# Attention kernel on one core: probabilities transposed by DMA, one per row tile, after the division, instead of by TensorE before it

## The chip, the cores and the metric

One Trainium2 chip, one NeuronCore of it. The metric is the device time of one execution in microseconds; of several runs the median is told. PE is TensorE, DVE VectorE, ACT ScalarE, POOL GpSimd and SP SyncE.

## The reference

For each of B = 8 images x of C = 128 channels and 32 x 32 = 1024 positions:

```python
h = group_norm(x, gn_w, gn_b)                     # 32 groups, eps 1e-5
hf = h.reshape(Bn, Cn, Hn * Wn)
q = jnp.einsum('bcn,oc->bno', hf, wq) + bq
k = jnp.einsum('bcn,oc->bon', hf, wk) + bk[None, :, None]
v = jnp.einsum('bcn,oc->bno', hf, wv) + bv
alpha = jnp.einsum('bnc,bcm->bnm', q, k) / jnp.sqrt(jnp.float32(Cn))
alpha = jax.nn.softmax(alpha, axis=-1)
out = jnp.einsum('bnm,bmc->bnc', alpha, v)
out = jnp.einsum('bnc,oc->bon', out, wo) + bo[None, :, None]
return out.reshape(Bn, Cn, Hn, Wn) + x
```

All in fp32.

## The kernel before

The weights are folded once: wq and wk into one matrix (u = its product with h), wo and wv into another (v already holds the output projection). Every fp32 operand of a large product is split into a high and a low fp16 part, and a product is three fp16 matmuls (high by high, high by low, low by high).

The scores of an image are 8 row tiles of 128 queries by 1024 keys (`TILES`); T = 8b + n numbers them over the launch, 64 in all. Four tiles are a group (`GT`), whose value products share one PSUM bank O. The steps of a tile:

- `logits` (PE, L470 to L474): six matmuls of 512 columns into S, one of two PSUM buffers.
- `tile_max` (DVE, L818): adds the keys' and queries' bias to S, writes the negative logits to SBUF and the row minimum (so the maximum) to exp_bias.
- `exponentials` (ACT, L669): exp into probs (fp32, two buffers in SBUF), the row sum beside it. The probabilities are not divided yet.
- `transposes` (PE, L534): eight fp32 transpositions of 128x128 from probs into the PSUM buffers pT0 and pT1.
- `high_parts` (ACT, L682) and `low_parts` (DVE, L828): from PSUM to the fp16 parts pT_hi and pT_lo, 512 columns at a time.
- `values` (PE, L497 to L499): six matmuls of 512 columns per step and four steps to a group, one group behind the tile.

The division comes at the end. `reciprocals` (DVE, L839 and L842) inverts the sums of four tiles at once; SP writes the 128x4 inverses to DRAM (L237) and reads them back broadcast over the partitions (L243); `result` on POOL multiplies (L367), then adds the residual xres (L375). For the last half group DVE does both (L946, L950).

Per image the other engines also make the next image's operands: DVE the statistics (`channel_stats`, L757, `group_spread`, `variance_out`, `group_affine`) and h itself (`normalise`, L804), POOL the split of h (L326, L329), of u (L336, L339), of v with c_tok (L346, L351, L354) and the residual (L358), ACT the copies of u, v and the products out of PSUM (L633, L643, L652).

There is no scheduler: each engine's program is written out in the order in which it runs, one `batch` per image with the steps hung on the tile number j, and semaphores (`wait_ge`) hold an instruction until its operands are there. DVE's order within a batch, for a tile j (shortened):

```python
tile_max(b, p, j + 1, first and j == 0)
if j == 0 and not first:
    reciprocals(b - 1, 1 - p, 1, second)
if j == 1 and not last:
    group_spread(b + 1, 1 - p)
...
    low_parts(b, j)
if j == 5:
    reciprocals(b, p, 0, first)
```

On every engine but SP the row maximum, exponential and logits of a tile stand one tile ahead of the transposition and split. SP issues all DMAs but two.

## Time and profile before

| | |
|---|---|
| median of 3 runs | 270.89 us (269.74 to 270.96) |
| profiled execution, its own time | 269.27 us |
| its span, first to last instruction | 267.5 us |
| PE busy | 254.0 us, 95% |
| DVE, ACT, POOL busy | 209.4, 176.3, 166.6 us |
| granted TensorE clock, mean | 0.995 |
| DMA traffic | 13.06 MB |

The span is what the trace covers. Busy is the time in which an engine works on an instruction; a matmul's end is modelled, so that busy PE is not PE at its peak. An instruction that is held inside its engine, by a port for instance, counts as busy for the whole of its time. Where an engine sat idle, the profile names what ended the wait.

### The profile page before, as it was taken

Reading aid. Unit: us, or ns where it says so; the run is one execution under the profiler, and the core shown is the slowest. Engines: PE = TensorE matmul, PEld = TensorE weight load, DVE = VectorE, ACT = ScalarE, POOL = GpSimd, SP = SyncE. Lnnn points to the kernel's source line nnn. Section 1 sums busy time; section 2 is a strip of 40 time slices with the busy share of each in tenths; the row PEclk is TensorE's granted clock in tenths of the full one; section 3 lists DMA queues with packets and bytes.
Section 4 is the critical chain, followed back from the end, with each engine's and each line's share of the span. In section 5 each row is a group of like instructions: output and inputs, shape, how many; then the busy total and the mean of one; then the engine's idle time right before and its main releaser. Section 6 shows DMA issues by size and latency. Waiting matters only on the chain.

```text
span 267.5 us, 5033 instructions
## 1 busy us (share of the span) xinstructions
PE 254.0 (95%) x1599; PEld 157.5 (59%) x1599; DVE 209.4 (78%) x403; ACT 176.3 (66%) x338; POOL 166.6 (62%) x182
## 2 busy tenths in 40 slices
PE   1979999999999999999999999999999999999992
PEld 1736555665666566566656666566556656665581
DVE  2757978988789778987789779887798788767742
ACT  2438777668666767677667767767776676767650
POOL 4047196545979099763988279772997359790621
PEclk9999999999999999999999999999999999999997
DMA  4202002130033102320033100420030200201034
GB/s 124 73 0 81 1 0 76 46 78 2 0 104 96 39 2 30 130 78 0 0 79 114 46 0 8 149 60 18 0 72 12 74 0 2 79 39 42 0 81 116
DMA packets 9808, 13.06 MB, mean 49 GB/s; under 512 B 3905, under 2 KB 4673, under 8 KB 9793
## 3 DMA queue, kind: packets, MB, share of 16 engines
q1 hardware_dynamic: 9504, 12.75, 17.1%
q14 instruction: 10, 0.07, 0.2%
q10 hardware_dynamic: 288, 0.13, 0.2%
q8 instruction: 6, 0.10, 0.2%
HBM read 8.65 MB, written 4.23 MB: 48 GB/s over the span
## 4 chain that ended last, share of the span: by engine, by line
PE 89%; DMA 4%; ACT 3%; DVE 2%; issue 1%; ACTq 0%; POOL 0%; DVEq 0%
PE pT L534 20%; PE S L470 10%; PE S L472 10%; PE S L474 10%; PE O L499 10%; PE O L498 10%; PE O L497 10%; PE misc L417 2%; PE misc L416 2%; PE misc L415 2%; ACT probs L669 2%; DMA wk_sb<-in_L_conv_wk_dram 2%; DMA inv_rows<-inv_line 1%; ACT pT_hi L682 1%; DMA inv_line<-row_inv 1%
## 5 line engine op out<-in xcount | busy, mean ns | idle before, releaser
L828 DVE SCALAR_TENSOR_TENSOR pT_lo<-pT,pT_hi 128x512 f16<-128x512 f32 x128 | 82.8, 684 | 21.4 <-ACT pT_hi L682 21.4
L682 ACT ACTIVATE pT_hi<-pT 128x512 f16<-128x512 f32 x128 | 69.5, 596 | 36.2 <-PE pT L534 35.5
L818 DVE TENSOR_SCALAR_CACHE_REDUCE neg_logits<-S,c_tok 128x1024 f32<-128x1024 f32 x64 | 81.8, 1279 | 13.3 <-POOL c_tok L346 8.0
L669 ACT ACTIVATE probs<-neg_logits,exp_bias 128x1024 f32<-128x1024 f32 x64 | 73.8, 1153 | 5.8 <-DVE neg_logits L818 5.7
L534 PE MATMUL pT<-ident,probs 128*128 128x128 f32 x512 | 66.7, 273 | 2.5 <-ACT probs L669 2.0
L534 PEld LDWEIGHTS pT<-ident,probs 128*128 128x128 f32 x512 | 58.9, 141 | 14.3 <-ACT probs L669 4.4
L497 PE MATMUL O<-pT_hi,v_hi 128*128 128x512 f16 x120 | 45.5, 379 | 0.0
L498 PE MATMUL O<-pT_lo,v_hi 128*128 128x512 f16 x120 | 45.5, 379 | 0.0
L499 PE MATMUL O<-pT_hi,v_lo 128*128 128x512 f16 x120 | 45.5, 379 | 0.0
L326 POOL TENSOR_TENSOR h_hi<-h,zero 128x512 f16<-128x512 f32 x14 | 14.6, 1041 | 47.0 <-DVE h L804 47.0
L470 PE MATMUL S<-h_hi,u_hi 128*128 128x512 f16 x128 | 38.5, 382 | 0.1
L472 PE MATMUL S<-h_lo,u_hi 128*128 128x512 f16 x128 | 38.5, 383 | 0.0
L474 PE MATMUL S<-h_hi,u_lo 128*128 128x512 f16 x128 | 38.4, 382 | 0.0
L367 POOL TENSOR_TENSOR attn<-av,inv_rows 128x512 f32<-128x512 f32 x15 | 23.3, 1555 | 6.9 <-DMA inv_rows<-inv_line 6.9
L336 POOL TENSOR_TENSOR u_hi<-u,zero 128x512 f16<-128x512 f32 x15 | 15.6, 1040 | 12.3 <-ACT u L633 12.3
L474 PEld LDWEIGHTS S<-h_hi,u_lo 128*128 128x128 f16 x128 | 12.6, 99 | 15.4 <-issue 0.6
L472 PEld LDWEIGHTS S<-h_lo,u_hi 128*128 128x128 f16 x128 | 12.6, 98 | 15.5 <-issue 0.6
L354 POOL TENSOR_TENSOR v_lo<-v,v_hi 128x384 f16<-128x384 f32 (+1 forms) x24 | 19.4, 809 | 1.9
L351 POOL TENSOR_TENSOR v_hi<-v,zeros 128x384 f16<-128x384 f32 (+1 forms) x24 | 20.4, 850 | 0.0
L375 POOL TENSOR_TENSOR y<-attn,xres 128x512 f32<-128x512 f32 x15 | 19.1, 1274 | 2.0
L497 PEld LDWEIGHTS O<-pT_hi,v_hi 128*128 128x128 f16 x120 | 11.7, 98 | 14.3 <-DVE pT_lo L828 2.3
L499 PEld LDWEIGHTS O<-pT_hi,v_lo 128*128 128x128 f16 x120 | 11.7, 98 | 14.2
(119 smaller groups left out, 313.3 us busy)
## 6 DMA issues: line engine op xcount, KB each, us to landing
inv_rows<-inv_line SPq DMA_DIRECT2D x16, 256.0 KB, 3.8
out_dram<-y SPq DMA_DIRECT2D x15, 256.0 KB, 2.0
x_sb<-in_x_dram SPq DMA_DIRECT2D x7, 512.0 KB, 3.3
x_sb<-in_x_dram SPq DMA_DIRECT2D x2, 256.0 KB, 3.6
inv_line<-row_inv SPq DMA_DIRECT2D x16, 2.0 KB, 1.4
out_dram<-y SPq DMA_DIRECT2D x2, 128.0 KB, 1.9
wq_sb<-in_L_conv_wq_dram ACTq DMA_DIRECT2D x1, 64.0 KB, 3.5
wk_sb<-in_L_conv_wk_dram ACTq DMA_DIRECT2D x1, 64.0 KB, 4.1
```

What stands on the lines that cost most here:

```text
L367: nc.gpsimd.tensor_tensor(by_tile(attn[:, q, :]), by_tile(av[:, q, :]), inverses(q), ALU.mult).then_inc(attn_done, 1)
L470: nc.tensor.matmul(s[:, c], q_hi, h_hi[:, p, c], start=True, stop=False)
L472: nc.tensor.matmul(s[:, c], q_hi, h_lo[:, p, c], start=False, stop=False)
L474: last = nc.tensor.matmul(s[:, c], q_lo, h_hi[:, p, c], start=False, stop=True)
L497: nc.tensor.matmul(O[:, :], vh, ph, start=(m == 0), stop=False)
L498: nc.tensor.matmul(O[:, :], vh, pl, start=False, stop=False)
L499: last = nc.tensor.matmul(O[:, :], vl, ph, start=False, stop=(m == TILES - 1))
L534: last = nc.tensor.transpose(pT[half][:, t, :], probs[:, n % 2, m * 128:(m + 1) * 128], ident[:, :])
L669: nc.scalar.activation(probs[:, n % 2, :], neg_logits[:, n % 2, :], ACT.Exp, scale=-1.0, bias=exp_bias[:, p, n:n + 1], accum_out=row_sum[: ...
L682: nc.scalar.activation(pT_hi[:, g, half * GT:(half + 1) * GT, n % GT, :], pT[half][:, :, :], ACT.Copy, scale=P_SCALE).then_inc(hi_done, 1)
L818: nc.vector.tensor_scalar(neg_logits[:, n % 2, :], S[n % 2][:, :], c_tok[:, p, n:n + 1], None, ALU.add, ALU.min, accum_out=exp_bias[:, p, ...
L828: nc.vector.scalar_tensor_tensor(out=pT_lo[:, g, ms, n % GT, :], in0=pT[half][:, :, :], scalar=P_SCALE, in1=pT_hi[:, g, ms, n % GT, :], op ...
```

## The change

The kernel is written anew in the parts around the probabilities; the head, the weights' folding and the three-matmul split stay.

- Removed: `transposes` and both pT buffers in PSUM, `spread_inverse` (32 DMAs), the product with the inverses on POOL, the loops (`Fori`); every engine's program is written out for all 8 images.
- `exponentials` as before. After it DVE's `inverse` scales the tile's row sum by 1/4096 and inverts it (128x1 each), ACT's `high_part` multiplies the tile by it into fp16 and DVE's `low_part` takes the rest, all from SBUF to SBUF over 1024 elements, into `parts`, one of four buffers of 128x2048 fp16.
- SP issues one transposing DMA per tile, 512 KB, from `parts` into `pT` (four groups), and `values` waits for the four of its group (`tr_in`), 7 tiles behind the logits (`LAG`).
- `low_part` lags one tile, `inverse` none. probs and neg_logits keep two buffers each.
- h of the next image is made on POOL, in `h_parts`. `result` on POOL is one addition. O and the bank for small products (M, before misc) are two each.

```diff
-            def transposes(b, n, first):
-                    for t in range(GT):
-                        m = half * GT + t
-                        last = nc.tensor.transpose(pT[half][:, t, :], probs[:, n % 2, m * 128:(m + 1) * 128],
-                                                   ident[:, :])
...
+            def transpose(b, n):
+                T = TILES * b + n
+                g = T // GT
+                eng.wait_ge(lo_done, T + 1)
+                if n % GT == 0 and g >= 4:
+                    eng.wait_ge(av_done, GT * (g - 3))
+                eng.dma_start_transpose(pT[:, g % 4, :, n % GT, :], parts[:, T % SPLITS, :]).then_inc(tr_in[n], 16)
...
+            def high_part(b, n):
+                T, p = TILES * b + n, b % 2
+                act.wait_ge(inv_done, T + 1)
+                if T >= SPLITS:
+                    act.wait_ge(tr_in[(T - SPLITS) % TILES], 16 * ((T - SPLITS) // TILES + 1))
+                nc.scalar.activation(parts[:, T % SPLITS, 0:N], probs[:, n % 2, :], ACT.Copy,
+                                     scale=row_inv[:, p, n:n + 1]).then_inc(hi_done, 1)
...
+            def inverse(b, n):
+                T, p = TILES * b + n, b % 2
+                dve.wait_ge(exp_done, T + 1)
+                nc.vector.tensor_scalar(scaled_sum[:, p, n:n + 1], row_sum[:, p, n:n + 1], 1.0 / P_SCALE, None,
+                                        ALU.mult).then_inc(sum_step, 1)
+                dve.wait_ge(sum_step, T + 1)
+                nc.vector.reciprocal(row_inv[:, p, n:n + 1], scaled_sum[:, p, n:n + 1]).then_inc(inv_done, 1)
+
+            def low_part(b, n):
+                T, p = TILES * b + n, b % 2
+                dve.wait_ge(hi_done, T + 1)
+                nc.vector.scalar_tensor_tensor(out=parts[:, T % SPLITS, N:2 * N], in0=probs[:, n % 2, :],
+                                               scalar=row_inv[:, p, n:n + 1], in1=parts[:, T % SPLITS, 0:N],
+                                               op0=ALU.mult, op1=ALU.subtract).then_inc(lo_done, 1)
...
+            for b in range(B):
+                for n in range(TILES):
+                    row_max(b, n)
+                    if n or b:
+                        low_part(b - (n == 0), (n - 1) % TILES)
...
+                    if n == 6 and b + 2 < B:
+                        channel_stats(b + 2)
+                        aggregate(b + 2)
+                    inverse(b, n)
...
+                nc.gpsimd.tensor_scalar(h[:, cols], x_sb[:, p, cols], ga[:, p:p + 1], gc[:, p:p + 1],
+                                        ALU.mult, ALU.add).then_inc(h_made, 1)
```

VectorE in the middle of an image before (L818 is the row maximum, L828 the low parts of the tile before it, L839 and L842 the inverses of four tiles):

```order
L818 TENSOR_SCALAR neg_logits,exp_bias<-S0,c_tok 128x1024 [waits exp_done,c_done,qk_done]
L828 SCALAR_TENSOR_TENSOR pT_lo<-pT0,pT_hi 128x4x128 [waits hi_done]
L828 SCALAR_TENSOR_TENSOR pT_lo<-pT1,pT_hi 128x4x128 [waits hi_done]
L839 TENSOR_SCALAR scaled_sum<-row_sum 128x4 [waits line_out0,exp_done]
L842 RECIPROCAL row_inv<-scaled_sum 128x4 [waits inv_step]
L818 TENSOR_SCALAR neg_logits,exp_bias<-S1,c_tok 128x1024 [waits exp_done,qk_done]
```

VectorE at the same place now (L698 is the row maximum, L714 the low part, L705 and L708 the inverse):

```order
L698 TENSOR_SCALAR neg_logits,exp_bias<-S0,c_tok 128x1024 [waits exp_done,qk_done]
L714 SCALAR_TENSOR_TENSOR parts<-probs,row_inv,parts 128x1024 [waits hi_done]
L705 TENSOR_SCALAR scaled_sum<-row_sum 128x1 [waits exp_done]
L708 RECIPROCAL row_inv<-scaled_sum 128x1 [waits sum_step]
L698 TENSOR_SCALAR neg_logits,exp_bias<-S1,c_tok 128x1024 [waits exp_done,c_done,qk_done]
L714 SCALAR_TENSOR_TENSOR parts<-probs,row_inv,parts 128x1024 [waits hi_done]
```

The two low parts of 512 have become one of 1024 whose first input is probs in SBUF, and the inverse stands behind every tile, where it waits for the exponential of the same tile; the next row maximum stands behind it.

ScalarE now, in the second image (L567 is the exponential, L578 the high part, L540 a copy of v):

```order
L578 ACTIVATE parts<-probs,row_inv 128x1024 [waits tr_in3,inv_done]
L567 ACTIVATE probs,row_sum<-neg_logits,exp_bias 128x1024 [waits lo_done,bias_done]
L540 COPY v<-M1 128x387 [waits v_done,v_mm]
L555 ACTIVATE ln_var<-var_eps 128x1 [waits var_out]
L557 ACTIVATE rstd0<-ln_var 128x1 [waits ln_step]
L578 ACTIVATE parts<-probs,row_inv 128x1024 [waits tr_in4,inv_done]
```

The high part of a tile stands ahead of the next exponential and waits for the tile's inverse and for the transposing DMA that read its buffer four tiles ago.

## Rows read from the trace of the kernel before

**Rows 1.** The page: span, and busy time, share and instructions of engines.

```profile
span 267.5 us, 5033 instructions
...
PE 254.0 (95%) x1599; PEld 157.5 (59%) x1599; DVE 209.4 (78%) x403; ACT 176.3 (66%) x338; POOL 166.6 (62%) x182
```

**Rows 2.** The page: chain that ended last, shares of the span by engine.

```profile
PE 89%; DMA 4%; ACT 3%; DVE 2%; issue 1%; ACTq 0%; POOL 0%; DVEq 0%
```

**Rows 3.** Busy time of each engine in a stretch in the middle.

```profile
core 0: us, PE busy (x) PEld busy (x) DVE busy (x) ACT busy (x) POOL busy (x), PEclk, DMA share, GB/s
124.00:155.00 31.00, 31.00 (x199) 19.03 (x198) 26.20 (x51) 21.58 (x41) 21.61 (x23) 1.00 0.19 51
```

**Rows 4.** Groups: busy us, mean ns of one | idle before, releaser.

```profile
L534 PE MATMUL pT<-ident,probs 128*128 128x128 f32 x512 | 66.7, 273 | 2.5 <-ACT probs L669 2.0
...
L757 DVE BATCH_NORM_STATS2 bn<-x_sb 128x6 f32<-128x512 f32 x15 | 9.7, 681 | 0.2 <-DMA x_sb<-in_x_dram 0.2
```

**Rows 5.** Timeline of one tile: start us, us, engine, what [idle before].

```profile
129.44 1.28 DVE L818 TENSOR_SCALAR_CACHE_REDUCE neg_logits<-S,c_tok 128x1024 f32<-128x1024 f32 x1 [1.34 <-POOL c_tok L346]
...
131.85 1.12 DVE L839 TENSOR_SCALAR scaled_sum<-row_sum 128x4 f32<-128x4 f32 x1
133.01 0.18 DVE L842 RECIPROCAL row_inv<-scaled_sum 128x4 f32<-128x4 f32 x1
...
131.79 1.16 POOL L339 TENSOR_TENSOR u_lo<-u,u_hi 128x512 f16<-128x512 f32 x1
...
130.85 1.15 ACT L669 ACTIVATE probs<-neg_logits,exp_bias 128x1024 f32<-128x1024 f32 x1 [0.46 <-DVE neg_logits L818]
131.91 0.19 ACT L669 ACTIVATION_READ_ACCUMULATOR probs<-neg_logits,exp_bias 128x1 f32 x1
```

**Rows 6.** Timeline, DVE and POOL around the two halves of h.

```profile
123.72 0.55 DVE L804 TENSOR_SCALAR h<-x_sb,ga,gc 128x512 f32<-128x512 f32 x1
...
125.98 0.92 DVE L804 TENSOR_SCALAR h<-x_sb,ga,gc 128x512 f32<-128x512 f32 x1
...
125.46 1.16 POOL L329 TENSOR_TENSOR h_lo<-h,h_hi 128x512 f16<-128x512 f32 x1
```

**Rows 7.** DVE instructions with two SBUF inputs: group of h_lo; timeline around spread.

```profile
L902 DVE TENSOR_TENSOR h_lo<-h,h_hi 128x512 f16<-128x512 f32 x2 | 1.3, 690 | 0.2 <-ACT h_hi L721 0.2
...
114.27 0.89 POOL L354 TENSOR_TENSOR v_lo<-v,v_hi 128x384 f16<-128x384 f32 x1
115.00 0.22 DVE L771 SCALAR_TENSOR_TENSOR spread<-dmean,mv 128x1 f32<-128x1 f32 x1
...
145.64 0.22 DVE L771 SCALAR_TENSOR_TENSOR spread<-dmean,mv 128x1 f32<-128x1 f32 x1
```

**Rows 8.** Groups of POOL that the change removes or that price what it adds.

```profile
L326 POOL TENSOR_TENSOR h_hi<-h,zero 128x512 f16<-128x512 f32 x14 | 14.6, 1041 | 47.0 <-DVE h L804 47.0
...
L367 POOL TENSOR_TENSOR attn<-av,inv_rows 128x512 f32<-128x512 f32 x15 | 23.3, 1555 | 6.9 <-DMA inv_rows<-inv_line 6.9
```

**Rows 9.** Timeline of DVE: first row maximum, last scaled sum, last y.

```profile
17.26 1.28 DVE L818 TENSOR_SCALAR_CACHE_REDUCE neg_logits<-S,c_tok 128x1024 f32<-128x1024 f32 x1 [2.63 <-POOL c_tok L346]
...
256.67 0.17 DVE L839 TENSOR_SCALAR scaled_sum<-row_sum 128x4 f32<-128x4 f32 x1 [0.33 <-ACT probs L669]
...
264.75 0.43 DVE L950 TENSOR_TENSOR y<-attn,xres 128x256 f32<-128x256 f32 x1
```

**Rows 10.** DMA: the queue (packets, MB, share); issues (KB each, us to landing).

```profile
q1 hardware_dynamic: 9504, 12.75, 17.1%
...
inv_rows<-inv_line SPq DMA_DIRECT2D x16, 256.0 KB, 3.8
...
x_sb<-in_x_dram SPq DMA_DIRECT2D x7, 512.0 KB, 3.3
```

More of the change, by code:

```diff
@@ L287, in _ @@
                               y[:, 1, cols]).then_inc(y_out[1], 16)
-            for q in range(2):
-                eng.wait_ge(line_out[q], 16 * B)
             for q in range(2):
@@ L340, in u_parts, with v_parts @@
                                         ALU.subtract).then_inc(u_done, 1)
-            def v_parts(b, p, part, first):
+            def v_parts(b, part):
+                p = b % 2
                 t0, n = V_PARTS[part]
@@ L347, in v_parts @@
                                         cb[:, :].to_broadcast([128, n]), ALU.add).then_inc(c_done, 1)
-                if part == 0 and not first:
+                if part == 0 and b >= 2:
                     eng.wait_ge(av_done, TILES * (b - 1))
@@ L398, in _ @@
[L398 to L409 removed]
+            v_parts(0, 0)
@@ new lines, in _ @@
+            eng.wait_ge(ob_out, 1)
+            residual(0)
+            for b in range(B):
+                v_parts(b, 1)
+                u_parts(b, 1)
+                if b + 1 < B:
+                    h_parts(b + 1, 0)
+                if b >= 1:
+                    result(b - 1, 0)
+                if b + 1 < B:
+                    h_parts(b + 1, 1)
+                v_parts(b, 2)
+                if b + 1 < B:
+                    u_parts(b + 1, 0)
+                    v_parts(b + 1, 0)
+                if b >= 1:
+                    result(b - 1, 1)
+                if b + 1 < B:
+                    if b >= 1:
+                        eng.wait_ge(y_done, 2 * b)
+                    residual(b + 1)
@@ L412, in _ @@
+            result(B - 1, 0)
         @block.tensor
@@ L439, in project_v @@
                 t0, n = V_PARTS[part]
+                if part or b:
+                    pe.wait_ge(v_out, NV * b + part)
+                if part == 1:
+                    pe.wait_ge(h_ready, 2 * b + 2)
                 for k in range(n):
                     tok = slice((t0 + k) * 128, (t0 + k + 1) * 128)
-                    last = split_product(bank[:, k * VW:(k + 1) * VW], h_hi[:, p, tok], h_lo[:, p, tok],
+                    last = split_product(M[1][:, k * VW:(k + 1) * VW], h_hi[:, b % 2, tok], h_lo[:, b % 2, tok],
@@ L457, in logits @@
                         pe.wait_ge(u_done, 2 * b + 1)
-                if n == 1 and first:
+                if n == 1 and b == 0:
                     pe.wait_ge(u_done, 1)
@@ L463, in logits @@
                     pe.wait_ge(u_done, 2 * b + 2)
-                if not first:
+                if T >= 2:
                     pe.wait_ge(bias_done, T - 1)
@@ L500, in values @@
[L500 to L514 removed]
+                    vh, vl = v_hi[:, p, m, 0:C], v_lo[:, p, m, 0:C]
@@ new lines, in values, with last_values @@
+                    ph, pl = (pT[:, 2 * p + q, part * TILES + m, :, :].rearrange("p t n -> p (t n)")
+                              for part in range(2))
+                    nc.tensor.matmul(O[q][:, :], vh, ph, start=(m == 0), stop=False)
+                    nc.tensor.matmul(O[q][:, :], vh, pl, start=False, stop=False)
+                    last = nc.tensor.matmul(O[q][:, :], vl, ph, start=False, stop=(m == TILES - 1))
+                last.then_inc(av_done, 1)
+            def last_values(half):
+                bank = (M[0], O[1])[half]
+                if half == 0:
+                    pe.wait_ge(u_out, 2 * B - 1)
+                else:
+                    pe.wait_ge(av_out, 2 * B - 2)
+                for t in range(GT // 2):
+                    pe.wait_ge(tr_in[GT + half * GT // 2 + t], 16 * B)
+                for m in range(TILES):
@@ L515, in last_values @@
                     vh, vl = v_hi[:, 1, m, 0:C], v_lo[:, 1, m, 0:C]
-                    ph, pl = (a[:, 1, m, LAST[half], :].rearrange("p t n -> p (t n)") for a in (pT_hi, pT_lo))
+                    ph, pl = (pT[:, 3, part * TILES + m, LAST[half], :].rearrange("p t n -> p (t n)")
+                              for part in range(2))
                     o = bank[:, 0:GN // 2]
```

552 lines of the change are left out of this document (190 added, 362 removed).

## The prediction

> **What bounds the kernel now.** I read the page's busy shares first: PE is busy 254.0 of 267.5 us, DVE 209.4, POOL 166.6 [rows 1]. The chain of waits agrees, with 89% of its time on PE [rows 2]. A stretch in the middle shows PE busy 31.00 of 31.00 us at full granted clock [rows 3]. So PE sets the pace: from the first row maximum at 17.26 to the last exponential's end, just before 256.67, 64 row tiles take 239.4 us, 3.74 us each [rows 9]. Of PE's work, 66.7 us are the fp32 transpositions of the probabilities at L534 [rows 4].
>
> **What leaves PE.** All 512 transpositions, 66.7 us. What is left is 254.0 - 66.7 = 187.3 us, some 2.9 us per tile. Logits and value products are the same in number and shape, so PE alone would allow 267.5 - 66.7 = 200.8 us. That would hold only if nothing else needed more than 2.9 us per tile. VectorE does.
>
> **The new loop of a tile.** The probabilities must be divided before they are split, so each tile now has a ring through two engines: row maximum of T (DVE), exponential of T (ACT), inverse of T (two tiny DVE instructions), and only then the next row maximum, because the inverse has no lag and stands in front of it on DVE. From the rows of one tile [rows 5]: the maximum begins at 129.44 and the exponential at 130.85, 1.41 us; the exponential with its accumulator read ends at 132.10, 1.25 us. At the end of the kernel, where POOL is idle, a scaled sum takes 0.17 us [rows 9]; a reciprocal takes 0.18 us [rows 5], of which some 0.1 us passes before the next instruction starts. With 0.06 us for the two handovers that is 1.41 + 1.25 + 0.06 + 0.17 + 0.10 = **3.0 us**.
>
> Beside the exponential runs the low part of T-1. Its inputs are both in SBUF and it covers 1024 elements. The nearest row, h_lo, takes 0.69 us for 512 [rows 7], the last y 0.43 for 256 [rows 9], so 256 elements cost 0.26 and 1024 take 0.69 + 0.53 = 1.22 us. It waits for the high part on ACT, 1024 elements, priced as the exponential's 1.15 us [rows 5]; this starts after the inverse and ends at about 1.3 us of the tile. Low part ends at 1.35 + 1.22 = 2.57; the exponential ends at 2.66. It is covered by 0.1 us and no more: whatever holds the low part up is paid in full.
>
> DVE's other work per batch: two bn_stats of 0.68 us [rows 4] and nine small instructions of about 0.2 us (such as the spread, 0.22 [rows 7]), 3.1 us, or 0.39 per tile; some 0.06 of it falls into the slack. ACT's copies of u, v and av stand between the exponential and the next high part, where DVE is busy for 1.4 us; I give their overhang 0.05. The ring with no contention is 3.0 + 0.33 + 0.05 = **3.38 us per tile**, above PE's 2.9: VectorE and ScalarE in turn take over the bound.
>
> **POOL.** It loses the product with the inverses (1.55 us, two per batch) and gets h, twice 512 elements, which I price as its h_hi of 1.04 us [rows 8]. The spread recurs after 145.64 - 115.00 = 30.6 us [rows 7], one batch; POOL was busy 21.61 us in 31 us [rows 3], or 21.3 in a batch, so it keeps about 21.3 - 3.1 + 2.1 = **20.4 us per batch**, all of it on SBUF.
>
> **Waits between DVE and POOL.** This is the term that decides. The scaled sum of 128x4, worth 0.17 us, takes 1.12 us where POOL's u_lo is in flight, and ends 0.02 us after it [rows 5]. The first half of h takes 0.55 us alone; the second takes 0.92, having met POOL's h_lo, and ends 0.28 us after it [rows 6]. DVE instructions of this kind, from SBUF to SBUF, wait for POOL's. Before, that struck 16 scaled sums and 7 halves of h. Now there are 64 scaled sums (of 128x1) and 64 low parts, whose main input was PSUM before and is SBUF now.
>
> - *Scaled sum.* Least: 0, if one element per partition takes another way. Most: the whole of the POOL instruction that was let in when the low part ended, about 1.0 us. POOL has work queued at that moment in roughly 8 of 10 tiles, since its 20.4 us must fit outside the 8 low parts: 20.4 / (8 * 4.5 - 8 * 1.22) = 0.78. I take 0.8 * 1.0 = **0.8 us**, since the 128x4 rows of the same instruction wait this way.
> - *Low part.* Least: 0; the spread, with two SBUF inputs, started at 115.00 while POOL's v_lo ran until 115.16 and still took its 0.22 us [rows 7]. Most: the rest of the POOL instruction in flight, on average half of 1.1 us, 0.55. I take the upper end, less the 0.1 us of cover and times 0.8: **0.37 us**. The spread touches only the last 0.16 us of a POOL instruction, while [rows 5, 6] meet one in its body and are SBUF to SBUF as the low part is.
>
> The Trainium skill speaks here against the change. Its page "SBUF — State Buffer", section "Who interferes with whom", says that a VectorE instruction with two SBUF inputs and a GpSimd instruction that reads SBUF exclude each other, the later waiting until the earlier has finished. No run here shows it for such an instruction; by it the low part waits, by the spread's row alone it doesn't, and the sum would be 315 us by the one and 270 by the other.
>
> **DMAs.** SP issues 64 transpositions of 512 KB. The 32 small DMAs for the inverses go. Rate: the queue moved 12.75 MB in 17.1% of 267.5 us, 0.28 MB per us [rows 10], so 0.52 MB would take 1.9 us, under the pace. The other end is the broadcast of 256 KB, 3.8 us to landing [rows 10], 7.6 us for twice as much if nothing overlaps. I take the lower end, since it is the rate of large transfers of the same queue. Four split buffers and four pT groups leave some 10 us from the low part to the reuse of its buffer, so a landing of 3.3 us, as for the 512 KB of x [rows 10], is hidden. SP's loads and stores queue between the transpositions; each waits for POOL's work of a batch earlier, so I cost them at nothing. The Trainium skill, page "DMA: Bandwidth & Descriptors", section "Latency and other measured facts", gives 261 GB/s for a transposing DMA into a non-contiguous destination, from which I estimate 2.0 us; no run here shows it yet, and by it the sum stays.
>
> **The sum.** Head until the first row maximum: 17.3 us, unchanged [rows 9]. Per tile 3.38 + 0.8 + 0.37 = 4.55 us; the last batch has little POOL work left, 3.5. So 56 * 4.55 + 8 * 3.5 = 282.8. Tail after the last inverse: high part 1.2, low part 1.3, DMA 3.3, 24 last products at half width 2.6, output 0.65 and its store 2.3 (265.18 to 267.5 [rows 9]): 11.4. Span 17.3 + 282.8 + 11.4 = 311.5. The profiled execution stood 1.8 us above its span (269.27), and the median (270.89) 1.6 above that execution: **315 us**.
>
> **Rivals.**
>
> - *B: only the low part waits.* Then DVE asks for less, but POOL's 20.4 and the low parts' 9.8 us need one another's absence, 30.2 us per batch, plus about 2 us in which POOL waits for ACT: 4.0 per tile, 17.3 + 224 + 28 + 11.4 + 3.4 = **284 us**. For it: 128x1 is a smaller shape than the rows that waited.
> - *C: only the scaled sum waits*, for the rest of a POOL instruction, 0.37 us: 3.75 per tile, **270 us**, no change.
> - *D, the other side: neither waits.* The ring of 3.38 us holds: 17.3 + 64 * 3.38 + 11.4 + 3.4 = **248 us**, faster. The place is the low part and the scaled sum on DVE; it decides as soon as their waits together stay under 0.35 us per tile (3.74 - 3.38). For it: reciprocal, bn_stats and spread never grew beside POOL. Against: [rows 5, 6].
> - *E: the transposing DMA sets the pace.* Beyond 4.55 us each it bounds everything, through the split buffers that the high part waits for. At the middle between 4.55 and 7.6, 6.1 us: 17.3 + 390 + 11.4 + 3.4 = **422 us**. For it: no transposing DMA has a row here, and it writes runs of 256 bytes.
>
> **Numbers.** My forecast (both wait) has 0.52, B 0.15, C 0.08, D 0.12, E 0.13. The forecast's own range is 295 to 345, from halving either wait or adding 0.5 us per tile. To hold 8 in 10 the range must take in B and C, the upper part of D's error and the start of E: 256 to 360. Under 0.5% (1.4 us) a measurement can't tell a change here. Faster by more: D and a third of C, 0.15. Within: 0.03. Slower: the rest, 0.82.
>
> **What would show it.** PE busy near 187 us and no longer the chain's main part; DVE and ACT alternating in the chain. The low part: 1.22 us where POOL is idle and up to 2.4 where it isn't, with its end a fixed step after POOL's. The scaled sum near 1 us in most tiles. POOL instructions stretched where they meet a low part. The transposing DMA landing within 10 us with no wait of ACT's high part on it. The forecast is wrong if low part and scaled sum keep 1.22 and 0.17 us beside a running POOL, or if the high part or PE waits for a transposition.

## The result, and the profile after

The changed kernel took 274.74 us (median of 4 runs, 273.76 to 275.07), the kernel before 270.69 on the same chip (4 runs): ratio 1.015, 95% interval 1.0114 to 1.0186. It is slower, as forecast, but by 4 us where 44 were forecast: 315 us was 40 too high, and inside the range only because that was wide (256 to 360). Where a kernel's runs fell into two groups, here and below, the ratio takes the faster group alone, so it can stand lower than the median suggests.

The page of the changed kernel (span, busy time, granted clock, queue, chain, the groups that matter; columns as in [rows 1, 2, 4, 10]):

```profile
span 272.1 us, 3536 instructions
...
PE 218.8 (80%) x1087; PEld 106.9 (39%) x1087; DVE 227.2 (83%) x419; ACT 181.4 (67%) x274; POOL 186.6 (69%) x181
...
PEclk9999795999979997799959997799979999799997
...
q1 hardware_dynamic: 138016, 42.09, 68.7%
...
DVE 34%; PE 34%; POOL 17%; issue 6%; ACT 5%; DMA 3%; SPq 0%; ACTq 0%; DVEq 0%
...
L698 DVE TENSOR_SCALAR_CACHE_REDUCE neg_logits<-S,c_tok 128x1024 f32<-128x1024 f32 x64 | 82.1, 1284 | 20.0 <-PE S L410 11.5
L714 DVE SCALAR_TENSOR_TENSOR parts<-probs,row_inv,parts 128x1024 f16<-128x1024 f32 x64 | 96.1, 1501 | 2.7 <-ACT parts L578 2.5
...
L346 PE MATMUL M<-mv,neg_mean_mat 128*128 128x1 f32 x16 | 4.4, 345 | 31.9 <-DVE mv L650 31.9
L262 POOL TENSOR_TENSOR h_lo<-h,h_hi 128x512 f16<-128x512 f32 x14 | 26.1, 1865 | 1.1
...
pT<-parts SPq DMA_TRANSPOSE x64, 3.7
```

PE is no longer the bound: its 66.7 us of transpositions are gone [rows 4], and DVE is the busiest engine. But PE's busy time fell only by 35.2 us, from 254.0 [rows 1] to 218.8, for two reasons. The busy times of PE's groups overlap, since a matmul begins before the one ahead of it has ended (one of 512 columns takes 0.38 us, and the next begins 0.22 us after it began): the records of all PE instructions but the transpositions cover 207.5 us of the trace of before, so at most 46.5 could go. And the clock that the throttle grants, at full speed in the stretch of [rows 3], now falls again and again. The queue carries 42.09 MB instead of 12.75 [rows 10], at 68.7% of the 16 engines, yet a transposition lands in 3.7 us.

The single instructions on DVE (duration in ns as min/median/max; first and last start):

```profile
L705 DVE TENSOR_SCALAR scaled_sum<-row_sum x64: 99/141/154, 20.3 to 258.1; 128x1 f32<-128x1 f32 x64
...
L714 DVE SCALAR_TENSOR_TENSOR parts<-probs,row_inv,parts x64: 1279/1338/2059, 21.8 to 259.7; 128x1024 f16<-128x1024 f32 x64
...
L683 DVE SCALAR_TENSOR_TENSOR gc<-neg_mean,ga,gb x8: 219/1196/1201, 9.5 to 212.9; 128x1 f32<-128x1 f32 x8
```

The scaled sum never waits, though 34 of the 64 lie wholly inside the time of a POOL instruction; the low part does wait, by up to 0.78 us; and the small `gc`, of one element per partition, is held up in seven of eight cases, by 0.7 to 1.0 us. The timeline shows with whom (start, duration, engine; around 86 us DVE, then POOL; around 100 us POOL, then DVE):

```profile
85.44 0.15 DVE L677 TENSOR_SCALAR newton<-newton 128x1 f32<-128x1 f32 x1
85.63 1.03 DVE L680 SCALAR_TENSOR_TENSOR ga<-rstd,newton,gw 128x1 f32<-128x1 f32 x1
86.69 1.20 DVE L683 SCALAR_TENSOR_TENSOR gc<-neg_mean,ga,gb 128x1 f32<-128x1 f32 x1
...
85.61 1.04 POOL L270 TENSOR_TENSOR u_hi<-u,zero 128x512 f16<-128x512 f32 x1 [1.41 <-ACT u L530]
86.72 1.16 POOL L273 TENSOR_TENSOR u_lo<-u,u_hi 128x512 f16<-128x512 f32 x1
...
98.59 2.10 POOL L262 TENSOR_TENSOR h_lo<-h,h_hi 128x512 f16<-128x512 f32 x1
...
102.10 1.04 POOL L270 TENSOR_TENSOR u_hi<-u,zero 128x512 f16<-128x512 f32 x1
...
98.39 1.28 DVE L714 SCALAR_TENSOR_TENSOR parts<-probs,row_inv,parts 128x1024 f16<-128x1024 f32 x1
...
100.95 1.28 DVE L698 TENSOR_SCALAR_CACHE_REDUCE neg_logits<-S,c_tok 128x1024 f32<-128x1024 f32 x1 [0.89 <-POOL c_tok L281]
...
102.16 2.06 DVE L714 SCALAR_TENSOR_TENSOR parts<-probs,row_inv,parts 128x1024 f16<-128x1024 f32 x1
104.14 1.27 DVE L644 BATCH_NORM_STATS2 bn<-x_sb 128x6 f32<-128x512 f32 x2
105.45 0.21 DVE L650 BATCH_NORM_AGGREGATE mv<-bn 128x2 f32<-128x12 f32 x1
...
111.48 1.28 DVE L698 TENSOR_SCALAR_CACHE_REDUCE neg_logits<-S,c_tok 128x1024 f32<-128x1024 f32 x1 [2.45 <-PE S L410]
```

`ga` and `gc` end with POOL's `u_hi` and `u_lo`. The low part at 102.16 waits for POOL's `u_hi`; the one at 98.39 was first, and POOL's h_lo, 1.16 us alone, takes 2.10. So the exclusion goes both ways, and nearly in full. The `spread`, whose row the prediction took as a sign that such an instruction may not wait [rows 7], waits too once it begins in the middle of a POOL instruction:

```profile
44.60 2.91 POOL L293 TENSOR_TENSOR xres<-x_sb,obias 128x1024 f32<-128x1024 f32 x1
45.93 1.60 DVE L659 SCALAR_TENSOR_TENSOR spread<-dmean,mv 128x1 f32<-128x1 f32 x1
```

And the statistics of the image after next (bn, mv) are there only at 105.7. PE stands in front of them, at the group mean; the windows (columns as in [rows 3]) show what that costs:

```profile
98.00:100.00 2.00, 2.00 (x11) 0.87 (x9) 1.93 (x5) 1.92 (x4) 1.92 (x2) 1.00 0.64 151
100.00:102.00 2.00, 0.36 (x2) 0.00 (x0) 1.11 (x2) 1.29 (x2) 1.92 (x4) 1.00 1.11 284
102.00:104.00 2.00, 0.00 (x0) 0.00 (x0) 2.00 (x3) 1.61 (x3) 1.92 (x3) 1.00 1.35 195
104.00:106.00 2.00, 0.28 (x2) 0.29 (x2) 1.93 (x7) 0.08 (x1) 2.00 (x3) 0.75 1.14 257
106.00:108.00 2.00, 2.00 (x7) 0.87 (x8) 2.00 (x3) 1.92 (x2) 1.19 (x2) 0.50 1.18 313
108.00:110.00 2.00, 2.00 (x7) 0.65 (x5) 0.97 (x6) 1.80 (x4) 1.05 (x1) 0.50 0.27 69
110.00:112.00 2.00, 2.00 (x13) 1.36 (x12) 0.52 (x1) 0.22 (x1) 1.92 (x2) 0.55 0.94 211
```

PE does 0.64 us of work in 6 us, then is granted half speed (0.50, the level of 1.2 GHz instead of 2.4) for some 6 us, with the work of that tile still to do; the next scores are late and DVE waits 2.45 us for them. This happens once in each image that has a group mean to make.

From the starts of the 64 row maxima (17.66 to 255.5) a tile takes 3.78 us in the mean, before 3.74. But the tiles differ: typically 3.2, **5.7**, 3.1, 2.9, 3.0, **3.8**, **4.9**, **4.4 to 5.7** us in an image of 31.1 us, and 2.9 to 3.0 from the third tile of the last image on, where POOL has little left. The ring of 3.0 us is there; four tiles of eight are far above it, each for a reason of its own. In the second stand `ga` and `gc`. At the end of the sixth DVE waits for POOL's key bias (c_tok, 0.89 us at 100.95). In the seventh are the low part of 2.06 us and the statistics. Behind the eighth the scores are late.

### The profile page after: what moved, and what is told of

It is laid out like the page before. It is cut to its first block, busy times and chain, and to the rows that moved or that the text cites. A ratio compares the mean times of both kernels' runs of the same rounds, so it can differ in the third digit from the quotient of the medians.

```text
span 272.1 us, 3536 instructions
## 1 busy us (share of the span) xinstructions
PE 218.8 (80%) x1087; PEld 106.9 (39%) x1087; DVE 227.2 (83%) x419; ACT 181.4 (67%) x274; POOL 186.6 (69%) x181
## 3 DMA queue, kind: packets, MB, share of 16 engines
q1 hardware_dynamic: 138016, 42.09, 68.7%
## 4 chain that ended last, share of the span: by engine, by line
DVE 34%; PE 34%; POOL 17%; issue 6%; ACT 5%; DMA 3%; SPq 0%; ACTq 0%; DVEq 0%
DVE neg_logits L698 13%; DVE parts L714 13%; POOL h_lo L262 5%; PE S L406 5%; POOL h L256 4%; PE O L430 4%; PE S L410 4%; PE S L408 4%; PE O L432 4%; PE O L431 4%; POOL h_hi L259 3%; DVE bn L644 3%; POOL y L303 2%; DVE gc L683 2%; ACT parts L578 2%
## 5 line engine op out<-in xcount | busy, mean ns | idle before, releaser
L578 ACT ACTIVATE parts<-probs,row_inv 128x1024 f16<-128x1024 f32 x64 | 73.4, 1146 | 42.1 <-DVE row_inv L708 42.0
L698 DVE TENSOR_SCALAR_CACHE_REDUCE neg_logits<-S,c_tok 128x1024 f32<-128x1024 f32 x64 | 82.1, 1284 | 20.0 <-PE S L410 11.5
L714 DVE SCALAR_TENSOR_TENSOR parts<-probs,row_inv,parts 128x1024 f16<-128x1024 f32 x64 | 96.1, 1501 | 2.7 <-ACT parts L578 2.5
L567 ACT ACTIVATE probs<-neg_logits,exp_bias 128x1024 f32<-128x1024 f32 x64 | 73.5, 1148 | 23.8 <-DVE neg_logits L698 20.5
L430 PE MATMUL O<-pT,v_hi 128*128 128x512 f16 x120 | 48.3, 402 | 0.5 <-DMA pT<-parts 0.5
L432 PE MATMUL O<-pT,v_lo 128*128 128x512 f16 x120 | 48.5, 404 | 0.0
L431 PE MATMUL O<-pT,v_hi 128*128 128x512 f16 x120 | 48.5, 404 | 0.0
L303 POOL TENSOR_TENSOR y<-av,xres 128x512 f32<-128x512 f32 x15 | 19.7, 1312 | 32.0 <-ACT av L549 32.0
L262 POOL TENSOR_TENSOR h_lo<-h,h_hi 128x512 f16<-128x512 f32 x14 | 26.1, 1865 | 1.1
L273 POOL TENSOR_TENSOR u_lo<-u,u_hi 128x512 f16<-128x512 f32 x15 | 24.2, 1614 | 1.2
L281 POOL TENSOR_TENSOR c_tok<-v,cb 128x3 f32<-128x3 f32 (+1 forms) x24 | 5.6, 232 | 25.0 <-ACT v L540 25.0
L406 PEld LDWEIGHTS S<-h_hi,u_hi 128*128 128x128 f16 x128 | 12.6, 104 | 25.5 <-issue 8.7
L432 PEld LDWEIGHTS O<-pT,v_lo 128*128 128x128 f16 x120 | 12.4, 103 | 16.1 <-issue 3.3
```

Of the source, the lines that this page charges most:

```text
L262: nc.gpsimd.tensor_tensor(h_lo[:, p, cols], h[:, cols], h_hi[:, p, cols], ALU.subtract).then_inc(h_ready, 1)
L303: nc.gpsimd.tensor_tensor(y[:, q, :], av[:, q, :], xres[:, b % 2, q * GN:(q + 1) * GN], ALU.add).then_inc(y_done, 1)
L406: nc.tensor.matmul(s[:, c], q_hi, h_hi[:, p, c], start=True, stop=False)
L430: nc.tensor.matmul(O[q][:, :], vh, ph, start=(m == 0), stop=False)
L431: nc.tensor.matmul(O[q][:, :], vh, pl, start=False, stop=False)
L432: last = nc.tensor.matmul(O[q][:, :], vl, ph, start=False, stop=(m == TILES - 1))
```

## The experiments

Ratios are to the kernel before on the same chip, with 95% intervals; `after` is the changed kernel, whose own ratio is 1.015. Differences from `after` in us are between medians that were measured on different chips. By the ratios, which set each run against the kernel before on its own chip, the second run gained 8 us and not 9, the third under 2 and not 2.5, and the fourth lost 11 and not 10; the others come out within 1 us, where nothing else is said.

**1. Statistics early.** x is loaded at tile 0 of an image instead of 2, and DVE makes the statistics at tile 4 instead of 6.

```diff
-                    if n == 2 and b + 2 < B:
+                    if n == 0 and b + 2 < B:
...
-                    if n == 6 and b + 2 < B:
+                    if n == 4 and b + 2 < B:
                         channel_stats(b + 2)
```

> Only the statistics move: the load of x is issued at tile 0 instead of 2, DVE's bn_stats and bn_aggr stand at tile 4 instead of 6. Theory 1 (PE, two tiles ahead, stands at the group mean until DVE's statistics of tile 6, 5.4 us per image, then works at half clock, and so delivers the scores of the next image's first tile 2.4 us late): the wait of PE on mv shrinks from 5.4 us to under 2, the granted clock rises from 0.918 to above 0.96, DVE no longer waits 2.4 us for S at the first tile, and the time falls by 6 x 2 to 6 x 3 us: 257 to 263. Rival (the ring of row maximum, exponential and inverse on DVE and ACT sets the pace everywhere, PE's wait is spare time): clock rises, time stays within 2 us of 274.7.

260.42 us, ratio 0.9649 (0.9583 to 0.9715): 14 us less than after. The mean granted clock rises from 0.918 to 0.959, and PE's waits for `mv` are gone from the top of its waits (us in total, times, longest):

```profile
PE S L406 <- issue: 14.2, 7, 2.4
PE M L352 <- DVE spread L659: 7.8, 8, 1.4
```

So the largest single loss that a run shows is where two steps stand. The rewrite had put them there. Before, DVE made the statistics of the next image at tile 0 and PE took the group mean behind the transpositions of tile 1, 3.5 us after `mv` was there (DVE, then PE, in before):

```profile
110.72 0.20 DVE L762 BATCH_NORM_AGGREGATE mv<-bn 128x2 f32<-128x12 f32 x1
...
114.42 0.28 PE L422 MATMUL misc<-mv,neg_mean_mat 128*128 128x1 f32 x2
```

Now both steps are made for the image after next, at tile 6 on DVE and behind the logits of tile 7 on PE, which no transposition holds back to DVE's pace. How much of the wait is from the new places and how much from PE being early, no run tells apart.

**2. PE kept busy.** 22 matmuls of 512 columns whose result nobody reads stand ahead of PE's wait for the statistics.

```diff
-                pe.wait_ge(stats, b + 1)
...
+                    for _ in range(22):
+                        nc.tensor.matmul(M[0][:, :], wu_hi[:, :], h_hi[:, b % 2, 0:HALF], start=True, stop=True)
+                pe.wait_ge(stats, b + 1)
                 nc.tensor.matmul(MEAN, neg_mean_mat[:, :]
```

> 22 matmuls of 512 columns whose result nobody uses are added on PE ahead of each of the six group means in the loop, about 4.7 us each time, so that PE is busy while it would wait for the statistics, which stay where they are. If the half clock after the wait is what makes the scores late: granted clock above 0.96, DVE's wait for S at the first tile of an image falls below 0.5 us, time falls by 12 to 18 us to 257 to 263. If the order alone does it (the mean stands ahead of the value products and the next scores): the clock rises and the time falls by less than 6 us.

265.63 us, ratio 0.9854 (0.981 to 0.9897): 9 us less than after, with more work on PE, and between the two expectations (12 to 18, and under 6). The windows show full clock where after had 0.50:

```profile
102.00:104.00 2.00, 1.52 (x8) 0.71 (x7) 1.92 (x6) 0.49 (x1) 1.92 (x4) 1.00 0.58 132
104.00:106.00 2.00, 2.00 (x11) 0.88 (x9) 2.00 (x5) 1.92 (x4) 0.87 (x1) 1.00 0.92 261
106.00:108.00 2.00, 1.96 (x17) 1.15 (x16) 1.93 (x8) 1.69 (x3) 1.38 (x2) 1.00 0.51 115
```

The last tile of an image falls from 4.4 to 5.7 us to 3.2. PE's wait itself costs little, since DVE doesn't need PE during it; what costs is that PE comes out of it at half speed. Part is given back: the second tile of the next image grows from 5.7 to 6.3. The run also explains PE's busy time: without the added matmuls its records cover 208.4 us, close to the 207.5 of before, so the low clock is what made it 218.8 in after.

**3. The small steps of the affine on GpSimd.** From the second image on, `ga` and `gc` are made by four 128x1 products and sums on POOL.

```diff
+                    eng.wait_ge(newton_done, b)
+                    g2(aff[:, p, 0:1], rstd0[:, p:p + 1], newton[:, p, 1:2], ALU.mult).then_inc(aff_step, 1)
...
+                    g2(gc[:, p:p + 1], aff[:, p, 1:2], gb[:, :], ALU.add).then_inc(affine, 1)
```

> From the second image on the last two 128x1 steps of the normalisation, ga and gc, run on POOL (four tiny tensor_tensor) instead of on DVE (two scalar_tensor_tensor with two SBUF inputs). Theory 2 (such DVE instructions wait for a POOL instruction that is in flight, however small they are: ga 0.71 and gc 1.02 us on the mean against 0.22): the second tile of each image shortens from 5.7 to about 4 us, time falls by 7 x 1.5 = 10 us to about 264. Rival (the 5.7 us tile is set by something else, such as the rate of ACT's copies): time stays within 2 us.

272.21 us, ratio 1.0088 (1.004 to 1.0136): 2.5 us less than after, where 10 were expected. The second tile falls from 5.7 to 3.45 us as hoped, but the sixth grows from 3.8 to 5.2, since POOL, later by its four steps, makes the key bias later:

```profile
DVE neg_logits L712 <- POOL c_tok L293: 18.7, 8, 3.1
```

after had 8.3 us of that. The delay changed its place.

**4. The scaled sum of four columns.** DVE's scaled sum takes 128x4 instead of 128x1, as the kernel before had it; nothing else that takes time differs.

```diff
-                nc.vector.tensor_scalar(scaled_sum[:, p, n:n + 1], row_sum[:, p, n:n + 1], 1.0 / P_SCALE, None,
+                k = n // GT * GT
+                nc.vector.tensor_scalar(scaled_sum[:, p, k:k + GT], row_sum[:, p, k:k + GT], 1.0 / P_SCALE, None,
```

> The scaled sum covers the four tiles of the group (128x4, as in the kernel before) in place of 128x1, 64 times; the reciprocal still takes one. Theory 3 (my forecast's 0.8 us per tile failed only because an instruction over one element per partition does not wait for POOL): the scaled sums take 0.16 to 1.3 us instead of 0.14, 0.5 us more on the mean, and the time rises by 20 to 40 us to 295 to 315. Rival (POOL is not in flight at that moment any more): they stay at 0.16 and the time within 3 us.

285.12 us, ratio 1.0564 (1.0514 to 1.0615): 10 us more than after, less than the 20 to 40 expected. The scaled sum, four of the tiny elements instead of one:

```profile
L709 DVE TENSOR_SCALAR scaled_sum<-row_sum x64: 153/170/1120, 20.4 to 271.4; 128x4 f32<-128x4 f32 x64
```

The first bound of the prediction's term (0, "if one element per partition takes another way") is the true one: the same instruction waits with four columns and doesn't with one. It also shows a second error. Even at four columns, 64 sums take 27.0 us in all, 17 above their 0.15; I had put 0.8 us on each, 51 us. Only 25 of the 64 took more than 0.2 us, and 16 more than 0.7. So POOL was not let in at the end of nearly each low part, as I had argued; why not, I did not follow up.

**5. The inverse lags too.** Inverse one tile behind, high and low part two, three buffers of probabilities.

```diff
-        probs = sb("probs", [128, 2, N], fp32)
+        probs = sb("probs", [128, 3, N], fp32)
...
-                    if n or b:
-                        low_part(b - (n == 0), (n - 1) % TILES)
+                    if n >= 2 or b:
+                        low_part(b - (n < 2), (n - 2) % TILES)
...
-                    inverse(b, n)
+                    if n or b:
+                        inverse(b - (n == 0), (n - 1) % TILES)
```

> The reciprocals lag one tile, the low part two, and the probabilities have three buffers; nothing else differs from the changed kernel. It takes the ring (row maximum, exponential, scaled sum and reciprocal of one tile) away and leaves every instruction. Theory 1 (the ring of some 3.0 us is the floor of the tiles, but in most images the time above it is DVE's own work, stretched where GpSimd reads memory beside it, and the late statistics): the last image, which runs at 2.9 to 3.0 us a tile, falls to DVE's busy time of some 2.9, and the others fall by 0.1 to 0.3 a tile, so 4 to 12 us less than the changed kernel (263 to 271). Theory 2 (the ring with its handovers is what each tile waits for, the missing lag of the inverse is the cost of the change): 20 us less or more (255 or below). Theory 3 (the inverse is never late): within 2 us of the changed kernel (273 to 277).

275.11 us, ratio 1.018 (1.0146 to 1.0213): no gain. The ring itself did get shorter, as theory 1 says: the last tiles of the last image take 2.73 to 2.79 us instead of 2.9. There DVE works without a gap, so this is the sum of its own instructions, only 0.15 us below the ring: in an undisturbed tile DVE alone is nearly the bound. But the parts are ready a tile later, and now the transposing DMA is late for PE, for which it waited 0.5 us in after at this line:

```profile
PE M L346 <- DVE mv L651: 28.5, 7, 4.9
PE O L430 <- DMA pT<-parts: 10.3, 10, 2.6
```

and the clock stays at 0.919. So theory 3 gave the right time for a reason it did not name: the lag buys 0.1 us in the few tiles that are at the ring, and costs a new wait.

**6 and 7. GpSimd without its work, and with memsets in its place.** From the third image on, each wide POOL instruction takes one column; the input's affine, the halves of h, u and v and the residual sum of these images are left out, and old values stand in. In the seventh run a memset of about the old duration stands ahead of each, which reads nothing.

```diff
+            def w(b, cols):
+                return cols if b < 2 else slice(cols.start, cols.start + 1)
...
-                cols = slice(half * HALF, (half + 1) * HALF)
+                cols = w(b, slice(half * HALF, (half + 1) * HALF))
...
+                filler(b, 950)
```

> From the third image on every wide GpSimd operation takes one column, so GpSimd neither reads much nor is late; the affine input, its halves, u, v and the residual sum of the images behind are left out (old values stand in). Theory 1 (what is above the ring in an image is GpSimd's: its reads stretch VectorE's low part and small steps, and its results come late; the late statistics and the low clock behind them stay in part): images 3 to 8 fall from 31 to 26 to 28 us, 6 x 4 = 24 us less than the changed kernel, 247 to 257, and the low part's mean in them is 1.28 us. Theory 2 (the exclusion is small, the statistics are everything): the images stay within 1 us, 268 to 275.

> The kernel with GpSimd's wide operations at one column, but each has a memset of about the duration of the original ahead of it (which reads nothing, and writes a tile that nobody reads); the same parts of the computation are left out. Theory 1 (GpSimd's reads exclude VectorE's two-input instructions, a memset doesn't): the low part stays at 1.28 us, but GpSimd's results are as late as before, so the time stands between the kernel with narrow operations and the changed one, 255 to 268. Theory 2 (any GpSimd work holds VectorE up): as the changed kernel, 272 to 277, low part 1.5 us. Theory 3 (lateness costs nothing, the reads everything): as the kernel with narrow operations, within 2 us.

246.71 us (245.61 to 250.78), ratio 0.9121 (0.9073 to 0.9169), and 253.0 us (248.38 to 258.82, a wide spread), ratio 0.9263 (0.9177 to 0.9348). With 270.09 us for the kernel before, these ratios are 246 and 250 us; the sixth is just below its range and the seventh below its 255. Their profiled executions lie above, with spans of 248.8 and 257.1 us, so I take only the durations of single instructions from them, and the differences from the ratios. The low part between 100 and 220 us, in after, the sixth and the seventh:

```profile
L714 DVE SCALAR_TENSOR_TENSOR parts<-probs,row_inv,parts x30: 1279/1532/2059, 102.2 to 218.7; 128x1024 f16<-128x1024 f32 x30
```

```profile
L741 DVE SCALAR_TENSOR_TENSOR parts<-probs,row_inv,parts x36: 1278/1283/1286, 102.1 to 218.9; 128x1024 f16<-128x1024 f32 x36
```

```profile
L741 DVE SCALAR_TENSOR_TENSOR parts<-probs,row_inv,parts x34: 1278/1283/1287, 99.7 to 219.0; 128x1024 f16<-128x1024 f32 x34
```

A POOL that works but reads next to nothing leaves the low part at 1.28 us in all 34 cases: it is the reading that excludes. So of the 28 us between after and the sixth, some 4 are POOL's results coming late (the intervals allow under 1 to 7), and some 24 its reads with what hangs on them, the low clock among it: the granted clock is 0.93 to 0.97 in their runs and 0.918 in after. The split is rough also because a POOL instruction that waits for a low part is late too; the two weren't parted further.

**8. Three moves at once.** Statistics early, affine on POOL, and the key bias of the last tiles ahead of the second half of h.

```diff
+                key_bias(b, 2)
                 if b + 1 < B:
                     h_parts(b + 1, 1)
                 v_parts(b, 2)
```

> Three things moved at once: x is loaded two tiles and the statistics are made two tiles earlier (as in the first run); the last steps of the affine are made on GpSimd (as in the third); and GpSimd makes the key bias of the last tiles ahead of the second half of h, not behind it. Theory 1 (in the third run the delay went from VectorE's two small steps to the key bias that GpSimd made later): with the bias moved ahead, both gains stand and add to the first run's: 260.4 less 4 to 10, so 250 to 257, and VectorE waits under 3 us for the key bias. Theory 2 (GpSimd's late work costs the same wherever it stands in its queue): no better than the first run, 258 to 263, with the wait at u's low half.

263.77 us, ratio 0.9739 (0.9679 to 0.98): no better than the first run alone, as theory 2 said; the ratios are 2 us apart and their intervals overlap. POOL is now busy 206.9 of 261.7 us and the chain is 50% POOL. More work on POOL did not pay in either order. Which of its instructions made the result late, this run does not show.

**9. The small steps without a second tensor.** The four 128x1 instructions of the group norm take their second and third operand as per-partition values; arithmetic and order are the same.

```diff
-                nc.vector.scalar_tensor_tensor(out=gc[:, p:p + 1], in0=neg_mean[:, p:p + 1],
-                                               scalar=ga[:, p:p + 1], in1=gb[:, :],
-                                               op0=ALU.mult, op1=ALU.add).then_inc(affine, 1)
+                nc.vector.tensor_scalar(gc[:, p:p + 1], neg_mean[:, p:p + 1], ga[:, p:p + 1], gb[:, :],
+                                        ALU.mult, ALU.add).then_inc(affine, 1)
```

> The four small VectorE instructions of the group norm that have two tensor operands in SBUF (spread, newton, ga, gc; 128x1 each) are written as tensor_scalar with the second and third operand given as one value a partition; the arithmetic is the same, and so is the place of each in the order. Theory 1 (what waits for GpSimd is a second tensor operand; an instruction with one and two per-partition values doesn't, as the scaled sum of 128x1 did not): gc falls from a mean of 1.02 us to 0.15 to 0.25, ga from 0.71 to the same; the second tile of an image falls by 1.0 to 1.8 us, and 7 images by 1 to 1.5 each: 264 to 270. Theory 2 (small operations of VectorE wait for GpSimd whatever their operands, and the scaled sum only never met it): gc stays at 1 us, 273 to 277. Theory 3 (the wait goes, but GpSimd's next result or the scores are late next, as in the third run): gc short, time 270 to 274.

268.71 us, ratio 0.9932 (0.9898 to 0.9967): 6 us less than after, and now a little faster than before.

```profile
L682 DVE TENSOR_SCALAR gc<-neg_mean,ga,gb x8: 271/272/274, 9.8 to 208.2; 128x1 f32<-128x1 f32 x8
```

A median of 1196 ns became 272, and none of the eight is above 274, though seven lie wholly inside the time of a POOL instruction; the second tile of an image falls from 5.7 to 4.1 us. Theory 1 holds.

**10. Both.** The rewritten steps on top of the early statistics of the first run.

> The same four instructions, on top of the early statistics of the first run (260.4 us). Theory 1: both gains add, since they are at different tiles of an image: 252 to 257. Theory 3 (another delay takes the place): 258 to 262.

**256.64 us, ratio 0.9514 (0.9478 to 0.9549).** The gains add in the main, as theory 1 said (256.6 in 252 to 257): the four steps are worth 4 us here and 6 alone. In the first run `ga` met no POOL instruction any more (220 ns at most), so there was less to gain. This is the fastest version that computes everything: 5% below the kernel before, 18 us below the changed one. Its longest DVE waits are for scores that PE begins late at two images' starts:

```profile
DVE neg_logits L696 <- PE S L410: 8.8, 7, 3.0
```

**11 and 12. ScalarE makes high halves; and with the lag.** On top of the tenth: ACT makes u's high half and v's of parts 1 and 2, straight from PSUM; the twelfth adds the lag of the fifth.

```diff
+                nc.scalar.activation(u_hi[:, b % 2, half * HALF:(half + 1) * HALF], M[0][:, :], ACT.Identity,
+                                     bias=ub[:, :]).then_inc(u_step, 1)
                 nc.scalar.activation(u[:, half * HALF:(half + 1) * HALF], M[0][:, :], ACT.Identity,
```

> On top of the kernel with early statistics and the four rewritten instructions: ScalarE makes the high half of u (15 of 128x512 from PSUM, 0.67 us each) and of v's parts 1 and 2 (16, some 0.5 us), which GpSimd made in 1.04 and 0.95 us; GpSimd's busy time falls by 30 us, ScalarE's rises by 18. Theory 1 (GpSimd's reads and its lateness are what is left above 2.9 us a tile, as the kernels with narrow operations show with 246.7): 3 to 8 us less than the kernel it builds on, 246 to 253. Theory 2 (ScalarE is in the ring: 18 us more on it lengthen the tiles by as much as GpSimd gives back): within 2 us of the kernel it builds on or slower.

> The same with the reciprocals lagging one tile, the low part two, and three buffers of probabilities. Theory 1 (with the late statistics and much of GpSimd's work gone, the ring of 2.9 us is next, and the lag takes 0.1 to 0.15 us a tile and ScalarE's added copies off it): 4 to 10 us less than the kernel before it. Theory 2 (the ring is not reached in most tiles even so, as the lag alone gave nothing on the changed kernel): within 2 us of it.

262.34 us (two runs at 258.1 and 258.6, two above 266, too far apart for an interval) and 266.0 us, ratio 0.9866 (0.9804 to 0.9927). The eleventh is 2 us worse than the tenth even by its two best runs, so theory 2 is the nearer; the twelfth is 9 us worse, which neither theory said. POOL's busy time fell from 203.9 to 149.9 us, but it now waits 38.3 us for ACT's u, and ACT's 13 us more lie in the ring. In the twelfth the transpositions are late again:

```profile
PE O L432 <- DMA pT<-parts: 21.6, 15, 2.9
```

## Why the prediction was right and wrong, point by point

- **PE loses its transpositions and the bound moves off it: right**, shown by the chain (DVE 34% where it had 2% [rows 2]). But "DVE and ACT alternating" is not what it shows: PE still has 34%, POOL 17% and ACT 5%. PE's remaining 187 us were wrong: 218.8. Some 20 of the 31 us are a wrong subtraction. The busy time of L534 overlaps its neighbours', and all else on PE covered 207.5 us before. The other 11 are the half clock behind the group means, since with the clock at 0.98 the same work covers 208.4 (second run).
- **The ring, 3.0 us: right.** Undisturbed tiles take 2.89 to 3.0. The low part is 1.28 us alone, not 1.22. DVE's own instructions need 2.74 of it (fifth run), so a full VectorE would have been nearly as good a name for the bound as the ring.
- **The scaled sum, +0.8 us a tile: the step that failed.** It took 0.10 to 0.15 us in 64 of 64 cases, where the sum had 0.8 us more. I judged the 128x1 instruction by its 128x4 row, though I had named the other bound. The fourth run shows both halves of the error: form (one column doesn't wait) and frequency (even four columns cost 0.28 us a tile, not 0.8; and of the 16 old ones, all of which the prediction counts as struck, 13 waited and three took 0.16 to 0.17 us). 45 us of the forecast stood on this term, 56 * 0.8. The Trainium skill, page "VectorE: DVE Perf Modes", section "Mode 2×_2P — use both read ports for one tensor", has the rule I should have read: an operation with one source, from SBUF to SBUF, uses both read ports only where its outermost dimension that isn't one is even, or odd and equal in source and destination; 128x1 has no such dimension. The traces agree with it (0.14 us beside a busy POOL against up to 1.12 for 128x4), but they show only the durations, not the ports.
- **The low part, +0.37 us a tile: mechanism right, size too large.** Mean 1.50 against 1.28 alone, +0.22. The seventh run shows that it is POOL's reads that do it. Of the two rows I weighed, the rule of the Trainium skill ("SBUF — State Buffer", section "Who interferes with whom") was the better guide than the spread's 0.22 us of [rows 7]: the trace and the seventh run agree with it, down to a memset, which doesn't read and doesn't exclude; the `spread` that took 1.60 us at 45.93 agrees too.
- **POOL, 20.4 us a batch: 23.3**, since the exclusion stretches POOL as well (h_lo 1865 ns in the mean, 1156 alone). I priced only DVE's side.
- **The nine small instructions at 0.2 us: wrong for two of them.** `ga` and `gc` have two tensor operands in SBUF, and now meet POOL's u halves: 0.7 and 1.0 us. Removing that wait gave 6 us (ninth run, all four steps rewritten). I applied the rule to the large new instruction only and not to the old small ones, whose company on POOL the change had altered.
- **Not foreseen: PE's wait for the statistics, with half clock behind it.** 14 us of the changed kernel's time (first run), of which the clock alone is most (8 to 9 us in the second). I asked what is late for DVE, and not for what PE, now with less work than a tile lasts, would have to wait; nor did I look at where the new order puts the statistics and the group mean.
- **DMA: right.** 3.7 us to landing against 3.3, hidden. Occupancy: 68.7% of 272.1 us is 187 us, 31 of them older traffic (17.1% of 267.5, less 4.2 MB of inverses), so 2.4 us for each transposition against my 1.9. The 261 GB/s of the Trainium skill (page "DMA: Bandwidth & Descriptors", section "Latency and other measured facts"; its words are a non-contiguous middle dimension, which here is the destination's) give an estimate of 2.0 us, nearer but also low; the measurement decides. Rival E is out; yet the fifth and twelfth runs show that there was only about one tile of room.
- **The rivals.** B (only the low part waits, 284 us) has the right mechanism, with 4.0 us a tile against 31.1 / 8 = 3.89 in the images where POOL works; but part of that 3.89 is the clock and the late statistics, which B did not have. C (270 us) is nearer in time and is refuted: the scaled sum, which it has waiting, does not wait, and the low part does. D (248 us) is about what the seventh run gives when POOL works on without its reads, 250: the exclusion decides between faster and slower, as the prediction said, but the missing 24 us were not all waits of the low part.
- **Head and tail: right**, the tail 2 us short. The first row maximum is at 17.66, the last at 255.5 of 272.1; from the last inverse, some 2.9 us later, 13.7 us are left against 11.4.

Errors of both signs met. Too much were 45 us for a wait that doesn't exist, 8 for the low part (56 * 0.15) and 4 for the last batch (8 tiles of 3.0 and not 3.5 us). Too little were 14 for PE's wait, 6 for the small steps and 2 for the tail: 315 - 57 + 22 = 280, where 274.74 was measured. The terms are not independent, and the last 5 us are not assigned; an undisturbed tile of 2.9 where the ring had 3.0 would be about as much. That slower came out is luck in part. Had I dropped the scaled sum's wait alone, the sum would have given 270, no change: the right sign rested on the wrong term.

## What to carry to other kernels

When a change takes work from the engine that set the pace, list what that engine will now wait for, in the order of the new program: what is made "just in time" for it may now be late, and here TensorE also came back from its long waits at half clock. Two lines that moved the load and the statistics by two tiles were worth 14 us, more than the 4 that the whole change had lost.

A VectorE instruction with a second tensor in SBUF waits for a GpSimd instruction that reads, even at 128x1 (here a `spread` of 0.22 us took 1.60); where the second operand is one value per partition, give it as one. Judge a wait by a row of the same form and shape, columns included, and count how often that row waited, not only how long it did once.

Lag is not free: a tile later out of the ring is a tile less for the DMA behind it (PE waited 10.3 us for it in the fifth run, 0.5 at the same line without the lag).

## What the hardware showed that I had not expected

- 128x1 against 128x4 of the same tensor_scalar beside a busy POOL: 99 to 154 ns always, against 153 to 1120 ns (25 of 64 above 200).
- A 128x1 instruction with two tensors in SBUF: 219 ns alone, 1201 ns at most for `gc` beside POOL and 1598 for `spread`; the arithmetic of `gc` with per-partition values 271 to 274 ns. It is 50 ns slower alone and up to 930 faster in company.
- After 6 us with 0.64 us of work PE was granted 0.50 of its clock for some 6 us of full work; 22 useless matmuls in that gap kept it at 1.00 and made the kernel 8 to 9 us faster.
- A transposing DMA of 512 KB takes 3.7 us to landing (3.6 to 6.9) and, by the queue's share, 2.4 us of all 16 engines. Beside 42 MB of traffic the others land a little later: stores of 256 KB in 2.7 us against 2.0 before, and loads of 512 KB in 4.3 against 3.3 [rows 10].
